# A decoder kernel's mixture stage: the last attention batch's tail dealt over thirteen expert pairs in place of eleven, and TensorE's part of it started one step in instead of three

## The chip, the cores and the metric

The kernel runs on one core of a Trainium2 chip. Each core has engines with queues of their own: TensorE (PE in the rows, its weight loads PEld), VectorE (DVE), ScalarE (ACT), GpSimd (POOL) and SyncE, which issues the transfers (SP). They run their queues in order and wait for each other on semaphores. The metric is the device time in microseconds, lower is better.

## The reference, cut to what matters

The program is a two-layer decoder over 4 batches of 512 tokens, width 128, in fp32. Six sublayers follow each other, each with a residual and a layer norm. The change lies where the second (cross attention, stage b) ends and the third (the mixture of experts, stage c) begins:

```
x = _layernorm(x + _L0_xattn_ref(ctx, x, ...))       # stage b: 16 heads of 64, then out @ Wo
x = _layernorm(x + _L0_ffn_ref(x, ...))              # stage c
...
logits = flat @ router_w.T                           # 16 experts
topk_scores, topk_idx = jax.lax.top_k(logits + router_bias, 2)
hidden = jax.nn.silu(gate_all) * up_all              # every expert, width 64
out = jnp.einsum('nk,nkd->nd', combine, down_all)    # plus one shared expert of width 128
```

## The kernel before, in words

Every engine's queue is written by Python generators. Each stage has a generator for each engine; a `yield` ends a step, and `weave` deals several generators out into one queue in proportion to numbers given by hand: `weave((g, n), (h, m))` takes from the one whose next step is the earlier by (steps taken + 1) / n. `later(n, g)` puts n empty steps ahead of g, `part(g, n)` takes only n steps of g, and `both` chains two.

Stage c works a batch in 9 pairs, p = 0 to 8 (`c_experts_*`). A pair covers two experts: on TensorE a gate and an up matmul, each 512 columns of fp32 (rows `c_gt` and `c_up`; `c_sg` and `c_su` for p = 8), and a matmul that spreads the routing weights over the partitions (`c_sel`, from `c_CT`). ScalarE makes the silu of the gate (`c_SG`, L1286), VectorE multiplies it by the up product (L1303, semaphore `c_su`) and then by the routing weight into `c_H` (L1309, semaphore `c_h`). Four down products per batch follow among the next batch's pairs (`c_dn`, L1329 adds them to X).

Between the pairs stands the routing of the next batch (`c_route_*`): logits (`c_rw`), L1213 and the picks up to L1217 on VectorE, an exp on ScalarE (L1205), then L1221 to L1235 on VectorE, which leave the one-hot weights `c_oh`; TensorE transposes these (L1199), and L1241 and L1243 make `c_CT` of them.

Into batch 0's pairs the tail of stage b is dealt, for the last attention batch (`b_out_*`): VectorE inverts the denominators (L966) and splits them in two fp16 halves (L972, L974, twice, `b_rp`). TensorE spreads them to eight tiles, a = 0 to 7, with two matmuls each (`b_rp,b_sel`); VectorE scales each tile of `b_OT` (L979, semaphore `b_sel`); TensorE multiplies by the output weights (`b_wo,b_OT`, 32 matmuls, semaphore `b_out`); VectorE adds to X and normalises (L236, L191 to L213); TensorE transposes the result (L221), which is needed by the fourth batch's routing and experts only.

PSUM banks come from a ring of six: `take` waits for the last reader of the bank's former content, so where a matmul stands in the queue also decides which semaphore it waits for.

Of the kernel before, what the change touches and what calls it, by code (L numbers as in the profile page):

```python
# [14 lines left out]
NB, T, D, TC = 4, 512, 128, 154  # L15
# [19 lines left out]
def weave(*streams):  # L35

    live = [[g, n, 0] for g, n in streams]
    while live:
        s = min(live, key=lambda s: (s[2] + 1) / s[1])
        s[2] += 1  # L40
        if next(s[0], StopIteration) is StopIteration:
            live.remove(s)


def part(gen, n):
    for _ in range(n):
        if next(gen, StopIteration) is StopIteration:
            return
        yield


def later(n, gen):
    for _ in range(n):
        yield
    yield from gen


def both(first, then):
    yield from first
    yield from then  # L60


def run(gen):
    for _ in gen:
        pass
# [60 lines left out]
def build(nc, io, phases=6):  # L126
    with ExitStack() as ctx:
        sems = {}

        def sem(name):  # L130
            name = SHARED.get(name, (name, 0))[0]
            if name not in sems:
                sems[name] = ctx.enter_context(nc.semaphore(name))
            return sems[name]
# [14 lines left out]
        ring = Ring(6)  # L149
# [8 lines left out]
        def mm(e, out, lhsT, rhs, start=True, stop=True):  # L158
            return e.matmul(out, lhsT, rhs, start=start, stop=stop, skip_group_check=True)  # L159
# [64 lines left out]
        def turn_tensor(t, s, b, banks=ring):  # L224

            bk = banks.take(t, ("turn", s, b), 1, "xt_" + s, b + 1)
            t.wait_ge("xr_" + s, b + 1)
            transpose4(t.e, bk, xb(b)).then_inc(sem("tp_" + s), 1)

        def turn_scalar(a, s, b):  # L230
            a.wait_ge("tp_" + s, b + 1)
            copy(a.e, XT[:, cols(b)], PS[:, bank["turn", s, b], :]).then_inc(sem("xt_" + s), 1)
# [707 lines left out]
        def b_out_tensor(t, b, banks=ringP):  # L940
            e, O = t.e, b_OT[b % 2]
            for _ in range(4):
                yield
            for a in range(8):
                bk = banks.take(t, ("bsel", b, a), 1, "b_sel", 8 * b + a + 1)
                t.wait_ge("b_rt", 2 * b + 2)
                mm(e, PS[:, bk, :], b_sel[:, a, :], b_rp[:, 0, :], stop=False)
                mm(e, PS[:, bk, :], b_sel[:, a, :], b_rp[:, 1, :], start=False).then_inc(sem("b_st"), 1)
                yield
            yield  # L950
            bo = banks.take(t, ("bo", b), 1, "b_add", b + 1)
            t.wait_ge("b_sel", 8 * b + 8)
            for j in range(4):
                for a in range(8):
                    last = mm(e, PS[:, bo, 128 * j:128 * j + 128], O[:, a, 128 * j:128 * j + 128], b_wo[:, a, :],
                              start=(a == 0), stop=(a == 7))
            last.then_inc(sem("b_out"), 1)
            for _ in range(12):
                yield
# [29 lines left out]
        B_OUT = 25  # L989
# [129 lines left out]
                    c_load_sync(s)  # L1119

        def b_tail_tensor(t):
            yield from later(3, b_out_tensor(t, NB - 1, ring))
            for _ in range(6):
                yield
            turn_tensor(t, "B", NB - 1)

        def b_tail_scalar(a):
            yield from later(3 + B_OUT + 6, ())
            turn_scalar(a, "B", NB - 1)

        def b_tail_vector(v):
# [203 lines left out]
        def c_order(lane, route, experts, tail, rows, turn, last, blocks, back):  # L1335


            begun = route(lane, 0)
            for _ in range(3):
                next(begun, None)  # L1340
            second = experts(lane, 1)
            weave((tail, B_OUT + 10), (both(experts(lane, 0, begun), part(second, 2)), 11))
            keys = both(rows(lane, 0), later(7, both(turn(lane, 0), both(blocks(lane), both(rows(lane, 1), later(16, turn(lane, 1)))))))
            weave((both(second, both(experts(lane, 2), experts(lane, 3))), 25), (later(46, keys), 112))
            run(back(lane, 0))
            for j in range(4):
                last(lane, NB - 1, j)
# [1075 lines left out]
        @block.tensor  # L2423
        def _(e):
            t = Lane(e, sem, "pe")
            a_tensor(t)
            b_tensor(t)
            if phases == 2:
                run(b_tail_tensor(t))
                return  # L2430
            c_order(t, c_route_tensor, c_experts_tensor, b_tail_tensor(t), lambda t, m: d_rows_tensor(t, m, ring),
                    lambda t, m: d_turn_tensor(t, m, ring), c_down_tensor, none, none)
            hidden = f_hidden_tensor(t, 0)
            d_order(t, d_chain_tensor, d_prep_tensor, lambda t, m: d_keys(t, d_rows_tensor, d_turn_tensor, m, ringD), d_late_tensor, e_first_tensor,
                    e_attend_tensor, none, c_last_tensor, none, none, lambda t, b: f_route_tensor(t, b, ringD), hidden)
            f_start_tensor(t)
            f_order(t, f_hidden_tensor, hidden, f_route_tensor, none, f_late_tensor)

        @block.scalar
        def _(e):  # L2440
            a = Lane(e, sem, "act")
            a_scalar(a)
            b_scalar(a)
            if phases == 2:
                run(b_tail_scalar(a))
                return
            c_order(a, c_route_scalar, c_experts_scalar, b_tail_scalar(a), d_rows_scalar, d_turn_scalar, none,
                    d_first_scalar, d_back_steps_scalar)
            hidden = f_hidden_scalar(a, 0)
            d_order(a, none, d_prep_scalar, lambda a, m: d_keys(a, d_rows_scalar, d_turn_scalar, m), d_late_scalar, e_first_scalar, e_attend_scalar,  # L2450
                    f_split_scalar, c_last_scalar, d_back_steps_scalar, d_blocks_steps_scalar, f_route_scalar, hidden)
            f_order(a, f_hidden_scalar, hidden, f_route_scalar, none, f_late_scalar)
# [152 lines left out]
```

## Time and profile before

| | us |
|---|---|
| median of 3 runs | 1805.92 |
| lowest, highest | 1803.56, 1810.51 |
| profiled execution, its own time | 1803.57 |
| its span | 1801.8 |
| TensorE busy, of the span | 1551.4 |
| VectorE busy | 1204.8 |
| first routing matmul of stage c starts at | 963.98 |
| stage b's output matmuls (`b_wo`), last batch | 996.58 to 1003.99 |

Times in the rows are microseconds from the span's start. The time lies 1.77 us over the span. A group of the timeline names the engine, the line, the operation and the tiles, output before input; fp32 matmuls count double, since each is run as two passes. In brackets stands how long the engine idled ahead of it and who ended that.

### The profile page before, as it was taken

The page shows a single profiled execution, that of the slowest core. Times are in us where ns is not written, and L with a number is a line of the kernel's source. Part 1 is how long each engine was busy: PE and PEld are TensorE (multiplying, and loading weights), DVE is VectorE, ACT ScalarE, POOL GpSimd, SP SyncE. Part 2 cuts the span into 40 slices and gives each one's busy share as a digit, 9 for nine tenths or more (in the row PEclk, how much of TensorE's full clock was granted, in tenths as well). Part 3 has the DMA queues.
Part 4 walks back from the last instruction along what each step waited for, and adds up shares of the span by engine and source line. Part 5 has one row for each costly group of instructions (what it writes and reads, how often), then busy time and mean ns, then how long its engine had stood idle before and what let it go on. Part 6 is the DMA issues. An engine that isn't in the chain of part 4 may idle for free.

```text
span 1801.8 us, 41198 instructions
## 1 busy us (share of the span) xinstructions
PE 1551.4 (86%) x17764; PEld 801.4 (44%) x17764; DVE 1204.8 (67%) x2337; ACT 907.4 (50%) x1258; POOL 667.7 (37%) x705
## 2 busy tenths in 40 slices
PE   4888877799999999999987888778988999798985
PEld 1222222233334333433422544567777778665542
DVE  6778875677775777567544567665576676565676
ACT  1676664367765776577574133335545444333220
POOL 1110110155654555466473003477555675100000
PEclk9899997799999999999998999999999999969998
DMA  4000002222231322223120100000000001100000
GB/s 146 1 1 1 1 1 79 68 68 83 70 98 53 106 68 68 69 84 89 48 68 13 62 1 1 13 3 15 15 15 15 15 3 47 49 2 1 1 13 12
DMA packets 32406, 70.61 MB, mean 39 GB/s; under 512 B 5328, under 2 KB 7056, under 8 KB 31968
## 3 DMA queue, kind: packets, MB, share of 16 engines
q1 hardware_dynamic: 32224, 67.98, 13.0%
q8 instruction: 140, 2.29, 0.6%
q14 instruction: 42, 0.34, 0.1%
HBM read 47.45 MB, written 20.51 MB: 38 GB/s over the span
## 4 chain that ended last, share of the span: by engine, by line
PE 57%; DVE 26%; ACT 6%; issue 5%; POOL 5%; DMA 1%; SPq 0%; DVEq 0%; ACTq 0%; POOLq 0%
PE ps L159 55%; DVE a_MX L371 4%; DVE b_mx L802 3%; POOL d_XI L1627 2%; POOL d_tmp L1624 2%; PE ps L221 1%; DVE d_KV L1519 1%; DVE b_VL L749 1%; POOL b_EL L874 1%; ACT d_L L162 1%; DVE st L165 1%; ACT d_XE L162 1%; DVE sq L200 1%; DVE st L191 1%; DVE X L197 1%
## 5 line engine op out<-in xcount | busy, mean ns | idle before, releaser
L874 POOL TENSOR_TENSOR b_EL<-b_X,b_EH 128x1024 f16<-128x1024 f32 x160 | 341.3, 2133 | 311.2 <-ACT b_EH L162 311.2
L802 DVE TENSOR_REDUCE b_mx<-ps 128x2 f32<-128x666 f32 x256 | 216.8, 847 | 103.3 <-PE ps L159 103.1
L1624 POOL TENSOR_TENSOR d_tmp<-d_G,d_XI 128x31 f32<-128x31 f32 (+15 forms) x248 | 130.1, 524 | 287.5 <-DVE d_G L1555 268.7
L856 ACT ACTIVATE b_X<-ps 128x1024 f32<-128x1024 f32 x160 | 163.8, 1024 | 131.1 <-PE ps L159 130.1
L162 ACT ACTIVATE b_EH<-b_X 128x1024 f16<-128x1024 f32 x160 | 169.1, 1057 | 27.9 <-PE ps L159 16.7
L408 ACT ACTIVATE a_E<-ps 128x1024 f32<-128x1024 f32 x128 | 131.2, 1025 | 102.8 <-PE ps L159 102.4
L371 DVE TENSOR_REDUCE a_MX<-ps 128x2 f16<-128x1024 f32 x128 | 155.3, 1226 | 39.6 <-PE ps L159 39.4
L159 PE MATMUL ps<-b_M,b_S 128*128 128x512 f16 (+1 forms) x768 | 176.6, 383 | 2.0 <-ACT b_X L856 2.0
L1627 POOL TENSOR_TENSOR d_XI<-d_XI,d_tmp 128x31 f32<-128x31 f32 (+15 forms) x248 | 140.9, 568 | 19.4
L159 PE MATMUL ps<-b_Hk,b_Hq 64*128 64x333 f16 x512 | 83.2, 322 | 39.9 <-DVE b_mx L802 36.9
L390 POOL TENSOR_TENSOR a_QS<-a_QS,a_MR 128x512 f16<-128x512 f16 x16 | 18.5, 1154 | 257.8 <-ACT a_MR L162 257.8
L159 PEld LDWEIGHTS ps<-b_Hk,b_Hq 64*128 64x128 f16 x512 | 24.7, 93 | 165.5 <-DVE b_mx L802 139.3
L159 PEld LDWEIGHTS ps<-b_M,b_S 128*128 128x128 f16 (+1 forms) x768 | 55.4, 97 | 76.7 <-issue 24.4
L2350 POOL TENSOR_TENSOR f_Y<-X,f_bo 128x512 f32<-128x512 f32 x4 | 6.1, 1536 | 202.9 <-DVE X L213 112.7
L159 PE MATMUL ps<-a_QS,a_KS 32*128 32x512 f16 x256 | 53.9, 418 | 27.9 <-DVE a_MX L371 26.8
L159 PE MATMUL ps<-f_XM,f_Wh 128*128 128x512 f16 x256 | 78.0, 387 | 0.0
L159 PE MATMUL ps<-a_E,a_VA 128*32 128x512 f32 x512 | 77.5, 681 | 0.4
L1286 ACT ACTIVATE c_SG<-ps 128x512 f32<-128x512 f32 x36 | 21.5, 597 | 110.2 <-PE ps L159 110.2
L159 PE MATMUL ps<-b_EH,b_VH 128*64 128x512 f16 x320 | 65.3, 404 | 5.0 <-POOL b_EL L874 2.7
L162 ACT ACTIVATE d_UW<-ps 128x512 f32<-128x512 f32 x64 | 38.0, 597 | 60.8 <-PE ps L159 60.6
L159 PE MATMUL ps<-d_KV,d_XE 64*64 64x128 f32 x1024 | 66.3, 279 | 1.2 <-issue 0.9
L159 PE MATMUL ps<-XT,a_w 128*128 128x512 f32 x64 | 47.5, 832 | 18.1 <-DMA ident<-ident 8.9
(305 smaller groups left out, 3321.4 us busy)
## 6 DMA issues: line engine op xcount, KB each, us to landing
b_S<-s_xk SPq DMA_DIRECT2D x48, 336.0 KB, 6.3
b_M<-s_xq SPq DMA_DIRECT2D x48, 256.0 KB, 5.1
s_xk<-b_Hk SPq DMA_DIRECT2D x16, 336.0 KB, 2.2
s_xk<-b_Lk SPq DMA_DIRECT2D x16, 336.0 KB, 2.5
s_xq<-b_Hq SPq DMA_DIRECT2D x16, 256.0 KB, 2.0
s_xq<-b_Lq SPq DMA_DIRECT2D x16, 256.0 KB, 2.0
d_XI<-eye SPq DMA_DIRECT2D x8, 512.0 KB, 3.8
f_w<-f_w SPq DMA_DIRECT2D x1, 2048.0 KB, 8.3
```

The costliest lines, as they stand in the source:

```text
L159: return e.matmul(out, lhsT, rhs, start=start, stop=stop, skip_group_check=True)
L162: return e.activation(out, a, ACT.Copy)
L165: return e.scalar_tensor_tensor(out=out, in0=a, scalar=s, in1=b, op0=op0, op1=op1)
L371: v.e.tensor_reduce(out, PS[:, bk:bk + 2, :], AX, ALU.max).then_inc(sem("a_mx"), 1)
L390: p.e.tensor_tensor(a_QS[G % 4], a_QS[G % 4], a_MR[G % 2], ALU.add).then_inc(sem("a_q2"), 1)
L408: a.e.activation(a_E[c][:, 2 * hp:2 * hp + 2, :], PS[:, bk:bk + 2, :], ACT.Exp, scale=float(D) ** -0.5).then_inc(sem("a_ex"), 1)
L802: v.e.tensor_reduce(out, PS[:, bk:bk + 2, 0:333], AX, ALU.max).then_inc(sem("b_mx"), 1)
L856: a.e.activation(b_X[k % 2], PS[:, bk:bk + 2, :], ACT.Exp, scale=0.125).then_inc(sem("b_ex"), 1)
L874: last = p.e.tensor_tensor(b_EL[k % 6], b_X[k % 2], b_EH[k % 6], ALU.subtract)
L1286: a.e.activation(c_SG[n % 3], PS[:, bank["cgu", b, p], :], ACT.Silu).then_inc(sem("c_sl"), 1)
L1624: e.tensor_tensor(tm, a, x, ALU.mult).then_inc(*p.step())
L1627: last = e.tensor_tensor(z, z, tm, ALU.subtract)
```

## The change

It edits four numbers of the weave and two of the tail. The tail's steps are dealt over 13 pairs (batch 0's nine and four of batch 1) in place of 11; the numbers of the weave behind it are lowered to match. TensorE's tail starts after one empty step in place of three, and ScalarE's copy of the transposed result moves with it; VectorE's tail has no such offset, before or after.

```
 def b_tail_tensor(t):
-    yield from later(3, b_out_tensor(t, NB - 1, ring))
+    yield from later(1, b_out_tensor(t, NB - 1, ring))
...
 def b_tail_scalar(a):
-    yield from later(3 + B_OUT + 6, ())
+    yield from later(1 + B_OUT + 6, ())
...
-    weave((tail, B_OUT + 10), (both(experts(lane, 0, begun), part(second, 2)), 11))
+    weave((tail, B_OUT + 10), (both(experts(lane, 0, begun), part(second, 4)), 13))
...
-    weave((both(second, both(experts(lane, 2), experts(lane, 3))), 25), (later(46, keys), 112))
+    weave((both(second, both(experts(lane, 2), experts(lane, 3))), 23), (later(37, keys), 103))
```

No instruction is added or taken away. On TensorE two things move. This is the first, from batch 1's logits, which stand behind pair 1, to the gate and up matmuls of pair 3 (`b_rp,b_sel` are the tail's spreading matmuls, two for each a; - is before, + is the changed kernel):

```order
 L159 MATMUL ps<-c_rw,XT 128x16 x4
 L159 MATMUL ps<-XT,c_gt 128x512 [waits c_su]
 L159 MATMUL ps<-XT,c_up 128x512
 L159 MATMUL ps<-c_CT_163,c_sel 128x512
-L159 MATMUL ps<-b_rp,b_sel 128x512 x2
 L159 MATMUL ps<-b_rp,b_sel 128x512 [waits b_sel]
 L159 MATMUL ps<-b_rp,b_sel 128x512
 L159 MATMUL ps<-b_rp,b_sel 128x512 [waits b_sel]
 L159 MATMUL ps<-b_rp,b_sel 128x512
-L159 MATMUL ps<-XT,c_gt 128x512 [waits c_su,c_lg]
+L159 MATMUL ps<-XT,c_gt 128x512 [waits c_lg,b_sel]
 L159 MATMUL ps<-XT,c_up 128x512
```

Ahead of these rows four of them stood, and now six do. So the tiles a = 0 to 7 stood as 2, 3, 3 behind pairs 1, 2 and 3; now they stand as 3, 2, 3, and the first matmul of pair 3 waits for `c_lg` (L1213) and an early `b_sel` and no more for `c_su` of pair 2. The second is the transpose L221, which moves from behind batch 1's pair 0 to behind its pair 2.

On VectorE the tail's instructions spread out. This is the place of pair 3, from pair 2's L1309 on; L979 scales the tiles of `b_OT`, and L236 is the tail's addition to X:

```order
 L1309 TENSOR_TENSOR c_H_168<-c_SG_166,ps 128x512 [waits c_wm,c_su]
-L979 TENSOR_TENSOR b_OT_101<-b_OT_101,ps 128x512 [waits b_st] x3
+L979 TENSOR_TENSOR b_OT_101<-b_OT_101,ps 128x512 [waits b_st] x2
 L1303 TENSOR_TENSOR c_SG_165<-c_SG_165,ps 128x512 [waits c_um,c_sl]
 L1309 TENSOR_TENSOR c_H_168<-c_SG_167,ps 128x512 [waits c_wm,c_su]
-L236 TENSOR_TENSOR X<-X,ps 128x512 [waits b_out]
-L191 TENSOR_REDUCE st<-X 128x4 [waits b_add]
-L193 TENSOR_SCALAR st<-st 128x4 [waits dve]
+L979 TENSOR_TENSOR b_OT_101<-b_OT_101,ps 128x512 [waits b_st] x2
 L1221 TENSOR_SCALAR c_wt<-c_wt 128x4 [waits c_ew]
 L1223 RECIPROCAL c_wt<-c_wt 128x4 [waits dve]
```

L979 stood three ahead of pair 3's L1303, and now two; and L236, which waits for `b_out`, stood ahead of L1221 and now doesn't.

Some rows on in the same queue, right behind pair 4's L1309, with pair 5's L1303 and L1309 in it:

```order
+L236 TENSOR_TENSOR X<-X,ps 128x512 [waits b_out]
+L191 TENSOR_REDUCE st<-X 128x4 [waits b_add]
+L193 TENSOR_SCALAR st<-st 128x4 [waits dve]
+L197 TENSOR_TENSOR X<-X,st 128x512 [waits dve]
 L1303 TENSOR_TENSOR c_SG_167<-c_SG_167,ps 128x512 [waits c_um,c_sl]
 L1309 TENSOR_TENSOR c_H_168<-c_SG_166,ps 128x512 [waits c_wm,c_su]
-L180 TENSOR_TENSOR st<-st 128x4 [waits dve]
-L165 SCALAR_TENSOR_TENSOR st<-st 128x4 [waits dve] x2
-L180 TENSOR_TENSOR st<-st 128x4 [waits dve]
-L165 SCALAR_TENSOR_TENSOR st<-st 128x4 [waits dve]
+L200 TENSOR_TENSOR sq<-X 128x512 [waits dve]
+L204 TENSOR_REDUCE st<-sq 128x4 [waits dve]
```

L236, L191 and L193 are here now, behind the whole of L1221 to L1235 and pair 4; L1241 and L1243, which make the next batch's `c_CT`, stand right behind these rows, now after L204 in place of further steps of the norm. Early in the tail one more thing moves: the first L972 and L974, which stood ahead of pair 0's L1303 and the first L1241 and L1243, now stand behind them. From batch 1's pair 2 on the order of each engine is as it was, but for the L221 and its copy on ScalarE. GpSimd's and SyncE's queues do not change.

## Rows read from the trace of the kernel before

**Rows 1.** The page, part 4: the chain that ended last, by engine.

```profile
PE 57%; DVE 26%; ACT 6%; issue 5%; POOL 5%; DMA 1%; SPq 0%; DVEq 0%; ACTq 0%; POOLq 0%
```

**Rows 2.** Waits of TensorE, 964 to 1023: us in total, times, longest.

```profile
PE ps L159 <- DVE c_SG L1303: 4.9, 2, 3.4
...
PE ps L1199 <- DVE c_oh L1235: 3.8, 2, 3.3
```

**Rows 3.** Windows: busy time of each engine by stretch; PEclk is the granted clock.

```profile
958.00:964.90 6.90, 4.43 (x49) 1.86 (x49) 1.35 (x4) 2.17 (x4) 4.85 (x3) 1.00 0.13 25
964.90:968.50 3.60, 3.56 (x6) 0.95 (x5) 2.84 (x23) 1.64 (x3) 0.00 (x0) 0.53 0.30 120
975.60:982.20 6.60, 6.51 (x16) 3.52 (x16) 2.57 (x4) 1.14 (x2) 0.00 (x0) 0.51 0.00 0
982.20:988.90 6.70, 3.34 (x11) 1.28 (x11) 4.54 (x20) 2.43 (x4) 0.00 (x0) 1.00 0.00 0
988.90:992.40 3.50, 3.50 (x8) 0.84 (x7) 0.74 (x2) 0.39 (x1) 0.00 (x0) 0.51 0.00 0
992.40:1006.00 13.60, 10.04 (x71) 7.99 (x69) 4.26 (x10) 0.60 (x1) 0.00 (x0) 1.00 0.07 17
1006.00:1012.60 6.60, 5.29 (x10) 2.09 (x11) 5.58 (x17) 0.60 (x1) 0.00 (x0) 0.50 0.96 334
```

**Rows 4.** Timeline of TensorE and VectorE, 975 to 1004: start, duration, idle before.

```profile
975.69 1.86 PE L159 MATMUL ps<-b_rp,b_sel 128*128 128x512 f16 x4 [0.49 <-DVE b_rp L974]
...
977.35 1.72 PE L159 MATMUL ps<-c_rw,XT 128*128 128x16 f32 x8
...
978.93 2.08 PE L159 MATMUL ps<-XT,c_gt 128*128 128x512 f32 x2
...
980.80 1.68 PE L159 MATMUL ps<-XT,c_up 128*128 128x512 f32 x2
...
982.73 1.47 PE L159 MATMUL ps<-b_rp,b_sel 128*128 128x512 f16 x6
983.37 1.88 DVE L979 TENSOR_TENSOR b_OT<-b_OT,ps 128x512 f32<-128x512 f32 x3 [3.90 <-PE ps L159]
985.17 0.22 DVE L1213 TENSOR_TENSOR c_lg<-ps,c_rb 128x64 f32<-128x64 f32 x1
...
986.74 0.68 DVE L1303 TENSOR_TENSOR c_SG<-c_SG,ps 128x512 f32<-128x512 f32 x1
...
987.56 1.10 PE L159 MATMUL ps<-XT,c_gt 128*128 128x512 f32 x2 [3.36 <-DVE c_SG L1303]
...
990.43 2.40 PE L159 MATMUL ps<-b_rp,b_sel 128*128 128x512 f16 x6
...
992.35 1.29 DVE L979 TENSOR_TENSOR b_OT<-b_OT,ps 128x512 f32<-128x512 f32 x2 [0.16 <-PE ps L159]
993.55 0.68 DVE L1303 TENSOR_TENSOR c_SG<-c_SG,ps 128x512 f32<-128x512 f32 x1
...
994.38 1.10 PE L159 MATMUL ps<-XT,c_gt 128*128 128x512 f32 x2 [1.55 <-DVE c_SG L1303]
...
996.58 7.41 PE L159 MATMUL ps<-b_wo,b_OT 128*128 128x128 f32 x64
```

**Rows 5.** Timeline of the same two engines, 1004 to 1023.

```profile
1004.03 0.69 DVE L236 TENSOR_TENSOR X<-X,ps 128x512 f32<-128x512 f32 x1 [9.20 <-PE ps L159]
...
1005.55 0.16 DVE L1221 TENSOR_SCALAR c_wt<-c_wt 128x4 f32<-128x4 f32 x1
...
1007.31 1.02 PE L1199 MATMUL ps<-ident,c_oh 128*16 128x128 f32 x4 [3.31 <-DVE c_oh L1235]
...
1015.45 1.10 PE L159 MATMUL ps<-XT,c_gt 128*128 128x512 f32 x2 [0.64 <-DVE c_CT L1243]
...
1022.12 0.66 PE L221 MATMUL ps<-ident,X 128*128 128x128 f32 x4
...
1022.61 0.61 PE L159 MATMUL ps<-c_dn,c_H 128*128 128x128 f32 x4
```


## Prediction

> **What bounds the kernel now.** I read the page first. In its chain TensorE has 57% and VectorE 26% [rows 1], so the kernel alternates between TensorE's own work and places where TensorE waits for VectorE; a time is changed only where one of these waits shrinks or grows. Next I asked for TensorE's waits in the stretch that the change touches. Two entries carry it: 4.9 us in two waits for `c_su` (L1303), the longest 3.4, and 3.8 us for `c_oh` (L1235), the longest 3.3 [rows 2]. Then the windows, for the clock: the granted clock is 0.51 from 975.6 to 982.2 and from 988.9 to 992.4, 0.50 from 1006.0 to 1012.6, and 1.00 between [rows 3]. These are the 1.2 and the 2.4 GHz level, and each of these falls comes shortly after TensorE stood idle for 3.3 us or more. So a long wait here is paid twice. An earlier fall, to 0.53 from 964.9, follows a stretch in which TensorE was busy for 4.43 of 6.90 us in several shorter waits [rows 3]. Last the timeline, which says who is in the way of whom.
>
> Pair 3's `c_gt` starts at 987.56 after 3.36 us of idle time, for pair 2's L1303 [rows 4]. That instruction had its operands from 982.4 on, but stood behind three L979 (983.37 to 985.25) and behind L1213 and the picks, so that it ran at 986.74. Pair 4's `c_gt` waits another 1.55 us, for pair 3's L1303 at 993.55, which again stood behind three L979. `b_wo` then runs 996.58 to 1003.99, all at the full clock. After it TensorE waits 3.31 us for `c_oh`: the exp for it was long done, but L1221 stands behind L236, which waits for `b_out`, and behind L191 and L193, so that it ran at 1005.55 [rows 5]. From 1007.31 TensorE works at half clock, and pair 7's `c_gt` starts only at 1015.45.
>
> **Part one: up to `b_wo`.** I replay the queues of the changed kernel with the durations of the rows.
>
> The recast L972 and L974 brings nothing: pair 0's `c_CT` comes some 0.7 us earlier, but both halves of `b_rp` are complete when they were, and TensorE's spreading matmuls need both. They start at 975.7 as before. There are now six of them ahead of `c_rw` in place of four. At half clock a spreading matmul takes 0.415 us (four from 975.69 to 977.35 [rows 4]), so `c_rw` starts at 978.2. It takes the 1.58 us that lay between 977.35 and 978.93, so pair 2's `c_gt` starts at 979.8, which is 0.85 us late. Its `c_su` of pair 1 has come by then, for only one L979 stands ahead of it. Gate and up and `c_sel` took 3.8 us, from 978.93 to the next spreading matmul at 982.73, nearly all at half clock; begun 0.85 us later more of it falls into full clock, and I put its end at 983.3.
>
> Now the gain. Behind pair 2 stand a = 3 and 4 alone. Tile 3 is spread at 983.8, its L979 follows until 984.6, since tiles 1 and 2 were scaled earlier, and L1213 gives `c_lg` at 984.85. Pair 3's `c_gt` needs this and `b_sel` of tile 2, no more pair 2's L1303, and starts at 984.95 in place of 987.56. The picks take the 1.57 us from L1213 to L1303 (985.17 to 986.74 [rows 4]), so pair 2's L1303 runs at 986.2, when its matmuls are long over, and the two L979 of tiles 4 and 5 end at 988.65, held by tile 5, whose matmuls start at 987.1 when the bank is free. Pair 3's L1303 runs 988.65 to 989.3 and pair 4's `c_gt` starts at 989.45, in place of 994.38. Gate to the end of `c_sel` is 2.2 us (994.38 to 996.58), so `b_wo` starts at 991.65; its last `b_sel` comes at 991.2. **Gain up to here: 996.58 - 991.65 = 4.9 us.** 2.6 us of it come from the wait that changes its partner (987.56 to 984.95). The other 2.3 come between the `c_gt` of pairs 3 and 4, 6.8 us before and 4.5 now: 0.9 from six spreading matmuls at full clock (1.47 us) in place of half (2.40 us), 0.7 from gate, up and `c_sel` (987.56 to 990.43, 2.9 us, now 2.2), 0.6 from a wait of 0.95 us in place of 1.55, since fewer L979 stand ahead of pair 3's L1303.
>
> **Part two: from the end of `b_wo` (call it T) to the first `c_dn`.** L1221 to L1235 take 1.65 us (1005.55 to about 1007.2 [rows 5]); they now stand in the 7.4 us in which `b_wo` runs and VectorE idled 9.2 us. Pair 4's L1303 and L1309 go there too. So TensorE goes from `b_wo` straight into the transposes, without the 3.31 us, and has no idle time for the clock to fall on. A pair at full clock is 2.22 us (three of them from 1015.45 to 1022.12, 6.67 us). After 0.44 us of transposes pairs 5 and 6 take until T + 4.9. Pair 7 waits for `c_ct`, and this is the new critical wait. VectorE starts at T with L236, L191 and L193, 1.52 us (1004.03 to 1005.55), and then has seven instructions of 0.69 us (L197, L1303, L1309, L200, L204, L1241, L1243; the size is that of L236 and L1303 in [rows 4, 5]), 4.8 us. With 0.15 us to TensorE's start, pair 7's `c_gt` starts at T + 6.5. Before it was 1015.45 - 1004.03 = 11.4 us behind T. The pairs 7, 8 and 0 behind it then run without a wait, as they did: pair 8's two last VectorE products end at T + 12.8, and `c_dn` comes at T + 6.5 + 6.67 = T + 13.2. L221, 0.49 us on TensorE between 1022.12 and 1022.61, only changes its place; there X is normalised at T + 13.7, while TensorE reaches L221 about T + 22. **Gain: 11.4 - 6.5 = 4.9 us.** The remaining idle time is 1.6 us at one place. I take it as too short for the clock to fall, since after the 1.55 us at 994.38 it stayed at 1.00 [rows 3, 4]; the price if it does fall is about 1.7 us, half of the 3.5 us stretch from 988.9.
>
> **What else moves.** The bank that L221 takes shifts the ring for a few pairs. The new waits there (pair 3 of batch 1 for pair 2's `c_su`, pair 4 for L221's copy) have a `c_dn` of about 2.1 us as cover, so I cost them at nothing; without that cover each would be below 1 us. The copy on ScalarE stands behind pair 2's silu, ahead of a table load; it can make pair 3's silu late by some 0.4 us, which VectorE's idle time there covers. The loads of the next stage wait for `b_out` and so start 4.9 us earlier; their stretch, DMA share 0.96 from 1006.0 on [rows 3], ends long before stage d. Everything from batch 1's pair 3 on keeps its order and moves as a whole.
>
> **Sum.** 4.9 + 4.9 = 9.8 us. Against the profiled execution's own 1803.57 us (span 1801.8) this is 1793.8. That execution was 2.35 us under the median of the runs; against the median, 1805.92, it is **1796.1 us**, 0.54% faster. A change of 0.5%, about what a measurement of this kernel can tell from none, is 9.0 us here: the forecast lies 0.8 us beyond it.
>
> **The rivals.**
>
> *The clock does not come back (slower).* The gains count on full clock for `b_wo` and the pairs behind it. No wait there is over 1.6 us, but before 964.9 shorter waits than that, 2.5 us of 6.9 in sum, were enough for a fall [rows 3]. The changed kernel has waits of 0.7, 0.1 and 0.95 us from 984 to 990, and one of 1.6 later. If TensorE stayed at half clock from `b_wo` up to L221's new place, `b_wo` would cost 7.4 us more and the work behind it (to T + 22, less the 1.6 us wait) 20.4 us more, of which the wait swallows 1.6: 26.2 us against a gain of 9.8, so 1822.3. It decides for slower than before once 9.8 us of full-clock work run at half, and for slower by over 0.5% at 18.8 us. For it speaks the fall at 964.9; against it that TensorE stays busy for some 80% from 984 to 990 (64% then), and that 1.55 us alone changed nothing. Chance 0.08, half of it for the over 0.5%.
> The Trainium skill, "TensorE: Matmul & The Clock Gate", section "A second HAM failure mode: psum-queue depth-cycling", says that frequent short idles between groups of matmuls that cycle through PSUM banks make the clock swing between its two levels; the changed kernel has such short waits, so by that rule it would go this rival's way, to some 1822 us by the same sum. The trace agrees at 964.9, where 4.43 of 6.90 us were busy and the clock went to 0.53, and not after the 1.55 us wait, where it stood at 1.00.
>
> *The first half is lost, within 0.5%.* Part one hangs on small margins: tile 5's matmuls, the exp with its two table loads on ScalarE ahead of pair 3's silu, and the late start of pair 2. If pair 4's `c_gt` is held 2 to 4 us more than I have, for instance because half clock lasts through pair 2 (0.6 us) and falls again in pair 3's stretch as it did at 988.9 (1.8 us), the gain is 5 to 9 us: 1797 to 1801. If only part two works it is 4.9 us, 1801.0. Chance 0.34.
>
> *The move does nothing.* If the slack is eaten later, because a chain that does not pass here sets the end, the time stays 1805.9. Against it: behind 1023 each engine's order is unchanged and nothing waits for a load. Chance 0.06.
>
> *More than forecast.* Six spreading matmuls with no pause could lift the clock ahead of 982.2. `c_rw`, `c_gt` and `c_up` at full clock would bring up to 2 us more: 1794. Chance 0.14, and 0.38 for the forecast proper.
>
> **How the numbers follow.** Faster by over 0.5% is the forecast and the larger gain, 0.38 + 0.14 = 0.52. Within is the lost first half, the move that does nothing, and half of the clock's rival, 0.34 + 0.06 + 0.04 = 0.44. Slower is the other half, 0.04. The range reaches from 1790, the larger gain and two times more the 1.7 us that a stretch of half clock costs, to 1803, where only part two works (1801.0) and one such stretch is added. The forecast's own range is 1794 to 1797.
>
> **What would show it.** In the profile after: pair 3's `c_gt` no more waiting for L1303, near 985; `b_wo` near 991.7; no idle time ahead of L1199 behind `b_wo`; pair 7's `c_gt` 6.5 us behind the end of `b_wo` with 1.6 us of wait for L1243; `c_dn` first near 1012.3 in place of 1022.6; granted clock 1.00 through that stretch. The prediction is wrong if the first two hold and the clock column shows 0.50 behind them, or if they hold and the span does not follow.

## The result, and the profile after

| | before | after |
|---|---|---|
| median of 8 runs each, us | 1806.77 | 1798.49 |
| lowest, highest | 1803.56, 1810.51 | 1789.21, 1802.61 |
| the profiled execution, us (span) | 1803.57 (1801.8) | 1791.45 (1789.5) |
| mean granted clock in it | 0.944 | 0.953 |

The ratio of the times is 0.9936, with a 95% interval from 0.9912 to 0.9960: 0.4% to 0.9% faster. The medians lie 8.3 us apart, the profiled executions 12.1. Forecast were 9.8 us and 1796.1 for the median, 1790 to 1803 as the range, and 1794 to 1797 as the forecast's own range; the median of 1798.49 lies in the wide one and not in the narrow one.

The eight executions lie 7 us apart before and 13 after, and part of what separates two profiled executions lies far from the change: about 320 us in, the one after was already 6.7 us ahead, with the same instructions. So I read the change from the part of the program that it touches. As a mark I use the first and the third L1199, the transposes for batch 1's and batch 3's routing; all that moved lies between them. First the two rows from the timeline of TensorE of the kernel before (start, duration, tile, idle time before), then the three of the kernel after.

```profile
968.92 0.60 PE L1199 MATMUL ps<-ident,c_oh 128*16 128x128 f32 x4 [0.46 <-DVE c_oh L1235]
...
1041.32 0.60 PE L1199 MATMUL ps<-ident,c_oh 128*16 128x128 f32 x4 [0.87 <-DVE c_oh L1235]
```

```profile
965.65 0.60 PE L1199 MATMUL ps<-ident,c_oh 128*16 128x128 f32 x4 [2.11 <-DVE c_oh L1235]
...
993.38 0.60 PE L1199 MATMUL ps<-ident,c_oh 128*16 128x128 f32 x4
...
1025.76 0.60 PE L1199 MATMUL ps<-ident,c_oh 128*16 128x128 f32 x4 [0.88 <-DVE c_oh L1235]
```

From the first to the third it is 1041.32 - 968.92 = 72.4 us before and 1025.76 - 965.65 = 60.1 after: **12.3 us saved, where the forecast had 9.8**. The second L1199 has no idle time ahead of it any more. That the profiled executions as a whole lie 12.1 us apart, nearly the same number, is chance: the one after was 3.3 us ahead at the first mark (965.65 against 968.92) and took 3.2 us more from the third mark to its end (763.7 against 760.5).

The waits of TensorE after, from 961 to 1010 (us in total, times, longest), which answer to [rows 2]:

```profile
PE ps L159 <- DVE c_CT L1243: 4.4, 2, 2.7
PE ps L1199 <- DVE c_oh L1235: 2.1, 1, 2.1
PE ps L159 <- DVE b_rp L974: 1.1, 1, 1.1
PE ps L159 <- DVE c_SG L1303: 0.7, 1, 0.7
PE ps L159 <- DVE c_lg L1213: 0.6, 1, 0.6
```

The 4.9 us for L1303 are 0.7, and the wait for `c_oh` that is left, 2.1, is the one ahead of the first L1199. Two waits grew: pair 7's for `c_CT`, 1.6 of the 4.4 us (before 0.6), and the one for `b_rp`, from 0.5 to 1.1; the first wait for `c_CT` shrank from 3.6 to 2.7. The windows, for the clock (PE, PEld, DVE, ACT and POOL busy, granted clock, DMA share, GB/s), which answer to [rows 3]:

```profile
965.60:971.60 6.00, 2.70 (x9) 1.07 (x9) 5.90 (x10) 0.67 (x2) 0.00 (x0) 1.00 0.00 0
971.60:975.00 3.40, 2.76 (x8) 1.33 (x9) 2.17 (x5) 0.00 (x0) 0.00 (x0) 0.50 0.00 0
975.00:986.13 11.13, 9.82 (x32) 3.79 (x32) 8.75 (x31) 4.56 (x6) 0.00 (x0) 1.00 0.00 0
986.13:993.50 7.37, 7.37 (x67) 7.33 (x67) 2.19 (x8) 0.00 (x0) 0.00 (x0) 1.00 0.01 2
993.50:1006.56 13.06, 11.43 (x31) 4.03 (x28) 12.10 (x30) 2.98 (x5) 0.00 (x0) 1.00 0.62 210
```

Half clock is left in one place, 971.6 to 975.0. Before it lasted twice as long there and came back twice more. And the timeline after, TensorE from the spreading matmuls to the first down products, which answers to [rows 4, 5]:

```profile
970.70 0.39 PE L159 MATMUL ps<-c_CT,c_sel 48*128 48x512 f16 x1 [2.74 <-DVE c_CT L1243]
972.24 2.72 PE L159 MATMUL ps<-b_rp,b_sel 128*128 128x512 f16 x6 [1.15 <-DVE b_rp L974]
974.75 1.09 PE L159 MATMUL ps<-c_rw,XT 128*128 128x16 f32 x8
975.69 1.10 PE L159 MATMUL ps<-XT,c_gt 128*128 128x512 f32 x2
...
979.51 1.10 PE L159 MATMUL ps<-XT,c_gt 128*128 128x512 f32 x2 [0.57 <-DVE c_lg L1213]
...
983.93 1.10 PE L159 MATMUL ps<-XT,c_gt 128*128 128x512 f32 x2 [0.74 <-DVE c_SG L1303]
...
986.13 7.41 PE L159 MATMUL ps<-b_wo,b_OT 128*128 128x128 f32 x64
...
999.89 1.10 PE L159 MATMUL ps<-XT,c_gt 128*128 128x512 f32 x2 [1.64 <-DVE c_CT L1243]
...
1006.56 2.27 PE L159 MATMUL ps<-c_dn,c_H 128*128 128x128 f32 x18
```

Pair 3's `c_gt` now waits 0.57 us and for L1213 in place of 3.36 for pair 2's L1303. It stands 13.9 us behind the first L1199 (before 18.6), pair 4's 18.3 (25.5), and `b_wo` 20.5 (27.7). So the first part brought 7.2 us. From the end of `b_wo`, 986.13 + 7.41 = 993.54, pair 7's `c_gt` is 6.35 us away and `c_dn` 13.0.

### The profile page after: what moved, and what is told of

Read it like the earlier page. It is cut to its first block, busy times and chain, and to the rows that moved or that the text cites. A ratio compares the mean times of both kernels' runs of the same rounds, so it can differ in the third digit from the quotient of the medians.

```text
span 1789.5 us, 41198 instructions
## 1 busy us (share of the span) xinstructions
PE 1546.2 (86%) x17764; PEld 805.1 (45%) x17764; DVE 1205.5 (67%) x2337; ACT 907.3 (51%) x1258; POOL 665.9 (37%) x705
## 4 chain that ended last, share of the span: by engine, by line
PE 58%; DVE 27%; ACT 7%; issue 5%; POOL 3%; DMA 1%; SPq 0%; DVEq 0%; ACTq 0%; POOLq 0%
PE ps L159 56%; DVE a_MX L371 4%; DVE b_mx L802 3%; PE ps L221 1%; POOL d_XI L1627 1%; POOL d_tmp L1624 1%; DVE d_KV L1519 1%; DVE b_VL L749 1%; POOL b_EL L874 1%; DVE st L165 1%; ACT d_L L162 1%; ACT d_XE L162 1%; DVE sq L200 1%; DVE st L191 1%; DVE X L197 1%
## 5 line engine op out<-in xcount | busy, mean ns | idle before, releaser
L162 ACT ACTIVATE b_EH<-b_X 128x1024 f16<-128x1024 f32 x160 | 169.1, 1057 | 27.9 <-PE ps L159 16.7
L1627 POOL TENSOR_TENSOR d_XI<-d_XI,d_tmp 128x31 f32<-128x31 f32 (+15 forms) x248 | 140.1, 565 | 19.4
L159 PE MATMUL ps<-b_Hk,b_Hq 64*128 64x333 f16 x512 | 82.7, 320 | 39.8 <-DVE b_mx L802 36.5
L159 PE MATMUL ps<-a_QS,a_KS 32*128 32x512 f16 x256 | 53.0, 411 | 27.7 <-DVE a_MX L371 26.6
```

The lines of the kernel that those rows point to most:

```text
L162: return e.activation(out, a, ACT.Copy)
L1627: last = e.tensor_tensor(z, z, tm, ALU.subtract)
```

## The experiments

In each of them the program outside the tail's stretch is that of the kernel it is made from. The table has, in us from the first L1199, where `b_wo` and the second and third L1199 start in the profile of each run, and how long the granted clock stayed at 0.5 in the stretch that began near 6.0 us (summed over short windows). The texts behind it take the runs one by one.

| run | made from | `b_wo` | second | third | half clock |
|---|---|---|---|---|---|
| before | | 27.7 | 38.4 | 72.4 | 6.8 |
| after | | 20.5 | 27.7 | 60.1 | 3.4 |
| after, second profile | after | 20.5 | 27.8 | 60.1 | 3.4 |
| after, third profile | after | 20.5 | 27.8 | 60.2 | 3.4 |
| add behind the routing | before | 27.6 | 34.8 | 67.8 | 6.8 |
| add ahead of the routing | after | 20.5 | 31.3 | 65.3 | 3.4 |
| filler in the wait for `c_oh` | before | 27.6 | 38.3 | 73.1 | 6.8 |
| filler ahead of the spreading | before | 29.1 | 39.8 | 73.4 | 10.2 |
| filler in the wait for `c_CT` | after | 20.6 | 27.9 | 60.2 | 3.4 |
| offset one alone | before | 23.6 | 35.8 | 70.4 | 6.8, from 2.5 |
| reciprocal ahead | after | 21.7 | 28.9 | 61.3 | 6.8 |
| more ahead of `c_rw` | before | 28.8 | 39.6 | 73.1 | 10.2 |
| more ahead of `c_rw`, reciprocal ahead | after | 21.1 | 28.4 | 60.8 | 3.4 |
| four edits | after | 21.6 | 28.8 | 59.9 | 6.8 |

The three profiles of the changed kernel agree within 0.1 us in every column, although these executions took 1791.45, 1795.03 and 1789.37 us: the stretch is the same each time, and differences of half a microsecond in it can be read. The kernel before has one profile, but the two kernels made from it that change nothing ahead of `b_wo` have it at 27.6 too, with 6.8 us of half clock. The other edits have one profile each.

The part behind the mark can be read too, from the same profiles. From the third L1199 to the end of the span it is 759.5 to 770.6 us, mean 765.0, in the six made from the kernel before (itself among them), and 758.9 to 770.7, mean 765.5, in the eight made from the changed one. So nothing shows that a later chain takes the gain back, though among such scatter a loss of a few us would not be seen.

**Part two alone.** L236 and what follows it on VectorE moved behind the routing and pair 4's products, TensorE's order left as before.

```diff
             yield
-            yield
+            yield from later(4 if b == NB - 1 else 1, ())
             v.wait_ge("b_out", b + 1)
```

> The kernel before, in which only L236 of the last `b_out` and the products behind it are moved behind pair 4's L1303 and L1309; TensorE's order is that of before. It is part two of the forecast alone. The measure is the distance from the first to the third L1199 of the stretch: 72.4 us in the profile of before, 60.1 in that of the changed kernel. My theory (two parts that add up): the wait for `c_oh` behind `b_wo` goes, 3.3 us, pair 7's `c_gt` comes 6.5 us behind the end of `b_wo` and `c_dn` 13.2 us behind it; the distance shrinks by 4.9 us, to about 67.5, and the whole time by 4.9 us, 0.27%. Rival (the first half brings everything, and part two's gain is eaten by the wait for `c_ct`): distance 72.4 to 71, whole time unchanged. Rival (half clock behind `b_wo` comes from the work of before it and not from the 3.3 us wait): half clock still shows from the transposes on, and pair 7 comes later than 8 us behind the end of `b_wo`.

Measured: ratio to before 0.9969 [0.9947, 0.9992], medians 1800.92 and 1806.28; the distance shrank by 4.6 us. TensorE from the end of `b_wo` on in this run:

```profile
990.06 7.41 PE L159 MATMUL ps<-b_wo,b_OT 128*128 128x128 f32 x64
997.31 0.60 PE L1199 MATMUL ps<-ident,c_oh 128*16 128x128 f32 x4
...
1004.42 1.10 PE L159 MATMUL ps<-XT,c_gt 128*128 128x512 f32 x2 [2.24 <-DVE c_CT L1243]
```

The wait for `c_oh` is gone, and pair 7 starts 7.1 us behind the second L1199 (after: 999.89 - 993.38 = 6.5). The 0.6 us more is three short VectorE instructions (L207, L174, L176) that stand ahead of L1241 in this order and behind L1243 in the changed kernel. My theory held (4.6 us for 4.9, pair 7 at 7.0 us behind the end of `b_wo` for 6.5), and both rivals fall.

**Part one alone.** The changed kernel with L236, L191 and L193 put back ahead of L1221.

```diff
                 e.tensor_tensor(O[:, a, :], O[:, a, :], PS[:, bank["bsel", b, a], :], ALU.mult).then_inc(sem("b_sel"), 1)
-                yield
-            yield
+                yield from later(0 if a == 7 and b == NB - 1 else 1, ())
+            yield from later(0 if b == NB - 1 else 1, ())
             v.wait_ge("b_out", b + 1)
```

> The changed kernel, with L236, L191 and L193 of the last `b_out` put back ahead of L1221, so that the routing waits for `b_wo` again. It is part one of the forecast alone. Forecast by its own sum: `b_wo` starts as early as in the changed kernel, the 3.3 us wait for `c_oh` is back with half clock behind it, and the distance from the first to the third L1199 is 72.4 less 4.9, 67.5 us (65 if part one is worth the 7.2 us that the profile after showed). Rival (part one's larger worth was an accident of that one execution's clock): 67.5 or more, with half clock up to about 982. Rival (the wait for `c_oh` alone carries the whole gain): 70 or more. Whole time 0.3% to 0.4% under before by my theory.

Measured: ratio to before 0.9964 [0.9941, 0.9988], medians 1797.27 and 1806.28; the distance 65.3, 7.1 us less than before. Behind `b_wo` it is the kernel before again:

```profile
994.79 1.02 PE L1199 MATMUL ps<-ident,c_oh 128*16 128x128 f32 x4 [3.31 <-DVE c_oh L1235]
```

The windows of TensorE in this run (busy, granted clock, DMA share, GB/s) over `b_wo` and the wait, and over what follows:

```profile
984.06:993.40 9.34, 7.41 (x65) 1.00 0.09 14
993.50:999.90 6.40, 5.11 (x10) 0.50 0.99 325
```

Part one is thus 7.1 us and part two 4.6, and 0.6 comes from having both (the three short instructions above): 12.3. That part one was worth more than 4.9 is no accident of one execution. By the whole times alone the two parts can't be told apart: 0.9969 and 0.9964.

**Is the wait for `c_oh` paid twice?** The kernel before, with TensorE kept at work in that wait.

```diff
-            t.wait_ge("c_oh", b + 1)
+            [mm(e, PS[:, bk, :], b_sel[:, 0, :], b_rp[:, 0, :]) for _ in range(14 * (b == 1))]; t.wait_ge("c_oh", b + 1)
```

> The kernel before, with 14 matmuls of 128 columns more, into the bank that the transposes will overwrite, ahead of the last wait for `c_oh`, so that TensorE is busy for part of that wait; their result is overwritten. If half clock behind `b_wo` comes from the idle 3.3 us, the granted clock stays at 1.00 from there on and the pairs behind take 2.2 us each in place of 2 x that: `c_dn` comes some 2 to 3 us nearer to the end of `b_wo` than in before (18.6 us), at 15.5 to 16.5. If half clock comes for another reason (the work ahead), the clock falls to about 0.5 all the same and the distance stays at 18.6 us or more.

```profile
1002.26 3.18 PE L159 MATMUL ps<-b_rp,b_sel 128*128 128x512 f16 x14
1005.73 0.60 PE L1199 MATMUL ps<-ident,c_oh 128*16 128x128 f32 x4 [0.29 <-DVE c_oh L1235]
...
1013.04 1.10 PE L159 MATMUL ps<-XT,c_gt 128*128 128x512 f32 x2 [2.43 <-DVE c_CT L1243]
```

The windows of the same run: the filled wait, pairs 5 and 6, and a stretch behind pair 7's start.

```profile
1002.30:1005.70 3.40, 3.14 (x16) 1.00 0.60 167
1005.70:1010.70 5.00, 4.88 (x14) 1.00 1.00 353
1014.40:1017.80 3.40, 3.40 (x6) 0.50 0.01 2
```

The added matmuls have 512 columns, as the rows show, and not the 128 that the expectation names. The clock theory held in this run: with the wait filled the fall behind `b_wo` is gone and pairs 5 and 6 ran at full clock. The gain that I expected of it did not come: `c_dn` starts 19.4 us behind the end of `b_wo`, where I had 15.5 to 16.5 and before it was 18.6. From the start of `b_wo` to pair 7's `c_gt` it is 18.0 us in place of 1015.45 - 996.58 = 18.9, because TensorE then waited 2.43 us for L1243 in place of 0.64; and behind that wait the clock fell once more, so that the whole distance came out 0.7 us longer. Up to pair 7, half clock behind `b_wo` cost the kernel before 0.8 us, since VectorE's chain to `c_CT` was right behind it. What part two gains, it gains for the most part by bringing that chain forward.

**The profile again.** No edit.

> The changed kernel once more, for a second profile. The profile after showed half clock only from 971.9 to 974.7 where I had forecast it until about 982, and `b_wo` 5.4 us earlier than forecast. Theory of the six spreading matmuls (they lift the clock because nothing interrupts them): again full clock from about the end of the first six on, and 20.5 us from the first L1199 to `b_wo`. Rival (where the clock turns is an accident of the execution): a different length of half clock, with the distance up to 25 us. Distance from the first to the third L1199: 60.1 by the first, 60 to 64 by the second.

The distance is 60.1, half clock 3.4 us long, `b_wo` at 20.5, one execution of 1795.03 us. The rival, an accident of the execution, falls. (Of the 5.4 us by which the expectation has `b_wo` too early, 3.3 lie ahead of the first L1199; by the mark it is 2.2.) Whether the six matmuls are the cause was still open.

**What decides how long half clock lasts?** Before and after begin to spread within 0.2 us of each other, and the one is at half clock twice as long. First the short gap ahead of the spreading matmuls in the kernel before, filled:

```diff
-                t.wait_ge("b_rt", 2 * b + 2)
+                [mm(e, PS[:, bk, :], c_sel[0:48, 0, :], b_sel[0:48, 0:4, :]) for _ in range(1 * (b == NB - 1 and a == 0))]; t.wait_ge("b_rt", 2 * b + 2)
```

> The kernel before, with one matmul of 512 columns more between the `c_sel` of pair 1 and the four spreading matmuls, in the 0.4 us in which TensorE waits there for `b_rp`; it writes the bank that the spreading matmuls overwrite. In before TensorE is at half clock for 6.9 us from 6.0 us behind the first L1199, in the changed kernel for 3.4 us only, though both begin to spread within 0.2 us of each other. Theory A (what TensorE does in the gap ahead of the spreading matmuls decides how long half clock lasts): with the gap filled the clock is back about 9.3 us behind the first L1199, as in the changed kernel, `c_rw` takes 1.1 us in place of 1.72 and pair 2's `c_gt` 1.1 in place of 2.08, so that `c_sel` of pair 2 ends some 2 us sooner. Theory B (it is the six in a row in place of four, or the earlier `c_sel`): half clock lasts until about 12.9 as before. In both pair 3's `c_gt` still waits for L1303, since that instruction stands behind three L979; its wait grows by what is won ahead of it under A only as far as VectorE isn't brought forward: distance from the first L1199 to `b_wo` 25.5 to 27.6.

Theory A is wrong, and B didn't foresee this either. `b_wo` came at 29.1, outside the 25.5 to 27.6 that I had for both, and the windows of TensorE show 10.2 us of half clock with the engine busy all through, and full clock only while it was idle again.

```profile
968.70:978.90 10.20, 10.20 (x24) 0.50 0.00 0
979.00:982.20 3.20, 0.42 (x2) 1.00 0.00 0
```

Next the long wait ahead of it in the changed kernel, filled:

```diff
-                    t.wait_ge("c_ct", b + 1)
+                    [mm(e, PS[:, 6, :], c_sel[0:48, 0, :], b_sel[0:48, 0:4, :]) for _ in range(10 * (b == 0 and k == 0))]; t.wait_ge("c_ct", b + 1)
```

> The changed kernel, with ten matmuls of 512 columns more (2.1 us) in the 2.7 us in which TensorE waits for the first `c_CT`; they write the bank that `c_sel` overwrites. If the fall of the clock 6.0 us behind the first L1199 comes from the idle time there, it goes: the six spreading matmuls take 1.5 us in place of 2.7, and `b_wo` starts 0.5 to 1.2 us sooner, 19.3 to 20 us behind the first L1199 in place of 20.5 (pair 2's `c_gt` can't start ahead of pair 1's L1303). If the clock falls all the same, 20.5.

The ten matmuls ran 2.33 us, which left 0.47 us of that wait and the 1.15 for `b_rp`. The clock fell all the same, at the same place, and nothing moved (distance 60.2). So the long wait isn't needed for this fall.

Then the six spreading matmuls 0.8 us sooner, by one reciprocal of the four placed ahead of the routing:

```diff
-                if q % 2:
+                if q % 2 or (b == NB - 1 and q == 0):
                     yield
...
-            begun = route(lane, 0)
+            begun = route(lane, 0); lane.name == "dve" and next(tail)
```

> The changed kernel with the first of the four L966 (0.85 us each) moved ahead of L1213, into the 0.77 us in which VectorE waits for the routing's matmuls. If what TensorE then waits for is VectorE's chain from the first L1235 to `b_rp`, `c_CT` and `b_rp` both come 0.8 us sooner and `b_wo` too: 19.7 us behind the first L1199 in place of 20.5, and the distance from the first to the third L1199 59.3 in place of 60.1. Rival (the clock then turns at another place, or the next wait takes it up): 60 to 62.

```profile
966.58 0.39 PE L159 MATMUL ps<-c_CT,c_sel 48*128 48x512 f16 x1 [1.92 <-DVE c_CT L1243]
968.11 2.62 PE L159 MATMUL ps<-b_rp,b_sel 128*128 128x512 f16 x6 [1.15 <-DVE b_rp L974]
970.53 1.73 PE L159 MATMUL ps<-c_rw,XT 128*128 128x16 f32 x8
972.10 2.05 PE L159 MATMUL ps<-XT,c_gt 128*128 128x512 f32 x2
```

Both waits ended 0.8 us sooner, as forecast, and the stretch came out 1.2 us longer: half clock lasted 6.8 us, with six spreading matmuls in a row as in the changed kernel. So the six in a row are not what brings the clock back early; my reading of the first profile falls, and the rival (the clock turns at another place) is right. The run gives a free test besides: it is the changed kernel with the long half clock that the prediction assumed. The prediction's 22.7 us to `b_wo`, less the 0.8, is 21.9, and 21.7 was measured.

The last theory was that `c_rw`, if it runs within the first part of half clock, keeps it long. Four matmuls more ahead of `c_rw` push it out, once in the kernel before and once in the run just told:

```diff
-            bk = ring.take(t, ("clg", b), 1, "c_lg", b + 1)
+            bk = ring.take(t, ("clg", b), 1, "c_lg", b + 1); [mm(e, PS[:, bk, :], c_sel[0:48, 0, :], b_sel[0:48, 0:4, :]) for _ in range(4 * (b == 1))]
```

> The kernel before, with four matmuls of 512 columns more between the four spreading matmuls and `c_rw` (8 in a row in place of 4). So far half clock lasted 3.4 us in the runs in which TensorE did only spreading matmuls until it ended (`c_rw` from 9.1 us behind the first L1199 on), and 6.8 or 10.2 in those in which `c_rw`, eight matmuls' records of 16 columns, ran ahead of that point (from 8.2 to 8.5 on), also with six spreading matmuls in a row. Theory C (`c_rw` inside the half-clock stretch keeps it long): with `c_rw` pushed to 9.3 us the clock is back at about 9.4, and pair 2's `c_gt` starts at 10.2 and takes 1.1 us. Rival D (the idle time ahead decides, which is as in before): half clock lasts 6.8 us or more and pair 2's `c_gt` starts at 10.9 and takes 2.1.

> The run with one reciprocal moved forward, and four matmuls of 512 columns more between the six spreading matmuls and `c_rw`, so that `c_rw` starts at 9.0 to 9.1 us behind the first L1199 in place of 8.2. Theory C: half clock lasts 3.4 us in place of 6.8, and `b_wo` starts 20.4 us behind the first L1199 in place of 21.7; distance from the first to the third L1199 60.0. Rival D: half clock lasts 6.8 us again and `b_wo` comes 0.5 to 0.8 us later than without them, at 22.2 to 22.5, distance 61.9 to 62.2.

In the kernel before it fails: `c_rw` starts at 10.4 us and half clock lasts 10.2.

```profile
979.50:989.70 10.20, 9.84 (x22) 0.50 0.00 0
```

Pair 3's `c_gt` then waited 3.36 us, as long as in the kernel before, and here the clock stayed at 1.00, from 989.8 to 1010.0:

```profile
994.63 1.10 PE L159 MATMUL ps<-XT,c_gt 128*128 128x512 f32 x2 [3.36 <-DVE c_SG L1303]
```

In the other it holds: half clock was 3.4 us long in place of 6.8, and `b_wo` came 0.5 us sooner than without the four, work added and time won, though at 21.1 and not at the 20.4 that I had. Windows of TensorE in that run:

```profile
973.50:976.90 3.40, 3.40 (x9) 0.50 0.00 0
977.00:988.00 11.00, 9.69 (x34) 1.00 0.00 0
```

Theory C explains one of two and is not enough. What decides between 3.4, 6.8 and 10.2 us of half clock stays open.

**One of the change's two choices alone.** The diff has five numbers of the weave and two of the tail, but only two choices stand behind them: thirteen pairs, and the offset of one step. Here is the offset with the eleven pairs of before.

```diff
-            yield from later(3, b_out_tensor(t, NB - 1, ring))
+            yield from later(1, b_out_tensor(t, NB - 1, ring))
...
-            yield from later(3 + B_OUT + 6, ())
+            yield from later(1 + B_OUT + 6, ())
```

> The kernel before with TensorE's and ScalarE's steps of the end of stage B one ahead in place of three, and the eleven pairs of before. VectorE's order is that of before. Tile 0 is now spread ahead of pair 1's `c_gt`, so that pair 1 waits until `b_rp` is there, 6.6 us behind the first L1199 in place of 0.4. By my theory (the two numbers only work together) this alone loses: pair 1's work, 1.9 us and its `c_su`, all comes behind `b_rp`, with half clock, and the first half is 1 to 4 us longer than before: 28.5 to 31.5 us from the first L1199 to the end of what stands ahead of `b_wo`; distance from the first to the third L1199 73 to 77. Rival (the offset is what gains): below 70.

```profile
970.66 1.04 PE L159 MATMUL ps<-b_rp,b_sel 128*128 128x512 f16 x2 [6.08 <-DVE b_rp L974]
971.49 1.92 PE L159 MATMUL ps<-XT,c_gt 128*128 128x512 f32 x2
```

Pair 1 waits 6.1 us, as I had said, and still the distance is 70.4, 2.0 us less than before and not more. The step that was wrong: I put all that follows at half clock. The clock fell 2.5 us behind the first L1199, inside the 6.1 us of idle time, where half clock costs nothing, and from 9.4 to 19.6 us all ran at the full one; and `b_wo` went ahead of pair 4, at 23.6, partly at half clock again (8.72 us for 7.41). So the offset alone gains 2.0 of the 12.3 us, in one profile. The other half, thirteen pairs with the old offset, was not tried, so what it would do alone stays open.

**Toward a better version.** The reciprocal as above; L1241 and L1243 ahead of L200 and L204; and both waits ahead of the spreading matmuls filled.

```diff
-            yield from normalize(v, xb(b), 1e-5, "xr_B", fine=True)
+            yield from (x for i, _ in enumerate(normalize(v, xb(b), 1e-5, "xr_B", fine=True)) for x in range(3 if b == NB - 1 and i == 1 else 1))
...
-                t.wait_ge("b_rt", 2 * b + 2)
+                [mm(e, PS[:, bk, :], c_sel[0:48, 0, :], b_sel[0:48, 0:4, :]) for _ in range(5 * (b == NB - 1 and a == 0))]; t.wait_ge("b_rt", 2 * b + 2)
...
-                    t.wait_ge("c_ct", b + 1)
+                    [mm(e, PS[:, 6, :], c_sel[0:48, 0, :], b_sel[0:48, 0:4, :]) for _ in range(8 * (b == 0 and k == 0))]; t.wait_ge("c_ct", b + 1)
```

> The changed kernel with four edits more: one L966 ahead of L1213; L1241 and L1243 of batch 1's table ahead of L200 and L204, so that pair 7's wait of 1.6 us for `c_CT` shrinks to 0.2; and 8 and 5 matmuls of 512 columns more in the waits for the first `c_CT` (1.9 us) and for `b_rp` (1.15 us), so that TensorE is nearly never idle between the first L1199 and the spreading matmuls. If the clock stays at 1.00 with both waits filled: `c_sel` 4.2 and spreading 5.8 us behind the first L1199, `b_wo` at 18.6 to 19.3 in place of 20.5, pair 7's `c_gt` 5.0 us behind the end of `b_wo` in place of 6.35, and a distance from the first to the third L1199 of 56.8 to 57.6 in place of 60.1. If the clock falls there all the same (as it did with the first wait alone filled): `b_wo` at 20.4 to 21.7, distance 58.7 to 60. Whole time 1.5 to 3 us under the changed kernel, too little to be told in the ratio.

> The changed kernel, timed beside the one with four edits more. Ratio to before 0.991 to 0.996 as in the first comparison, median 1797 to 1800; distance from the first to the third L1199 60.1 us, half clock there 3.4 us long.

Timed together: with four edits more 0.9919 [0.9889, 0.9949] of before, median 1787.81 of 6 runs; the changed kernel 0.9930 [0.9908, 0.9952], median 1790.17 of 10; before 1804.44. The intervals overlap, so the ratios don't tell the two apart. For the changed kernel the ratio, the distance and half clock came as expected; the median, for which I had 1797 to 1800, came 7 us lower. In the stretch the edits cancel. Pair 7's wait is 0.31 us, so the table ahead of the square brought its 1.3 us:

```profile
997.29 1.10 PE L159 MATMUL ps<-XT,c_gt 128*128 128x512 f32 x2 [0.31 <-DVE c_CT L1243]
```

But `b_wo` came at 21.6 in place of 20.5. With both waits filled TensorE was busy for 3.55 of the 3.64 us ahead, and the clock fell and stayed down for 6.8 us:

```profile
965.51:969.15 3.64, 3.55 (x16) 1.00 0.00 0
969.20:972.60 3.40, 3.40 (x13) 0.50 0.00 0
972.60:976.00 3.40, 3.40 (x6) 0.50 0.00 0
```

Of the four, L1241 and L1243 ahead of the square is the one to keep; alone on the changed kernel it was not run.

## Why the prediction was right

**The ratio.** Forecast 0.54% faster, measured 0.64%, by medians 8.3 us for 9.8. The forecast's chance of 0.52, for faster by over 0.5%, lay on the side that came, but narrowly: the interval reaches from 0.4% to 0.9%, and the medians taken by themselves give 0.46%. The mark in the trace says 12.3 us. The two comparisons (0.9936 and 0.9930, 11.6 and 12.6 us) agree with it, but their intervals hold the forecast's 9.8 as well, so it is the mark alone that tells the two apart. By it, what came is the rival "more than forecast" (0.14) and not the forecast proper (0.38).

**Part one, the mechanism.** Each step came where it was put: `c_rw` behind six spreading matmuls, pair 3's `c_gt` held by L1213 and no more by pair 2's L1303, pair 4's `c_gt` 4.4 us behind it (forecast 4.5), held by L1303 for 0.7 us (forecast 0.95).

**Part one, the size.** The mis-sized term is the clock: the prediction kept half clock up to about 982, as before, and so had pair 3's `c_gt` 16.0 us behind the first L1199 and `b_wo` 22.7; measured were 13.9 and 20.5. Half clock lasted 3.4 us and not 6.8, so `c_rw`, gate and up of pair 2 ran at the full clock. That is 2.2 us in three profiles of three, the size that the rival "more than forecast" gave it (up to 2). Its reason, six spreading matmuls with no pause, is refuted as a cause by itself by the run with the reciprocal ahead. So part one is 7.1 for the forecast 4.9, and the sum 12.3 for 9.8; of the 2.5 us that the sum is short, this one term is 2.2. That the clock is its cause is shown by the run with the reciprocal ahead, which has the long half clock and comes out at the prediction's sum.

**Part two.** Forecast 4.9 us, pair 7's `c_gt` at 6.5 behind the end of `b_wo` and `c_dn` at 13.2, with 1.6 us of wait for L1243. Measured 6.35, 13.0 and 1.64, and 4.6 for the part alone, 5.2 on top of part one (65.3 to 60.1). The prediction's opening said that "a long wait here is paid twice". For this one that was wrong in effect: the filled wait took the half clock away and gained 0.8 us up to pair 7. The sum didn't rest on it, since it was taken from VectorE's chain. The reading behind it, that each fall comes shortly after 3.3 us or more of idle time, doesn't hold either: behind `b_wo` the clock fell at 1006.0, 2.0 us into the wait; near 6.0 us behind the first L1199 it fell also with the waits there filled (four edits); and with four matmuls more ahead of `c_rw` in the kernel before, pair 3's 3.36 us of idle time left it at 1.00.

**The rivals.** The clock that does not come back did not happen: after waits of 0.57, 0.74 and 1.64 us the granted clock stayed at 1.00 up to 1006.56. The Trainium skill's section "A second HAM failure mode: psum-queue depth-cycling" in "TensorE: Matmul & The Clock Gate" would have it swing there; in this stretch it did not. The first half was not lost, which had 0.34; the move did not do nothing.

## What to carry to other kernels

Where one engine waits for an instruction that was ready long before it ran, look at what stands ahead of it in its queue: changing which instruction a wait hangs on (3.4 us to 0.6), and moving a chain into the time another engine's long matmul leaves idle (3.3 us to none), can be priced by replaying the queues. The second part was worth what the replay said (4.6 to 5.2 us for 4.9); the first was worth 2.2 us more (7.1 for 4.9), because the replay had to assume when the clock comes back. A half clock or a wait is worth removing only if the next engine isn't right behind it; replay that one too before counting it. And where executions scatter by more than the edit is worth, compare distances between two marks in the traces: here these agreed within 0.1 us over three profiles while the eight times of the changed kernel lay up to 13 us apart.

## What the runs showed of the hardware that was not expected

- Near the change, stretches of half clock came out 3.4, 6.8 or 10.2 us long in these profiles, and a small edit changed which: six spreading matmuls begun 0.8 us sooner turned 3.4 into 6.8 (`b_wo` 1.2 us later), and four useless matmuls more turned that back to 3.4 (`b_wo` 0.5 us sooner).
- In these runs a busy TensorE wasn't safe from the fall. With 3.55 of 3.64 us busy, mostly matmuls that contract over 48 rows, the clock fell (four edits); with 3.14 of 3.40 us busy, with matmuls over 128 rows, it stayed at 1.00 (filler in the wait for `c_oh`). Both runs in which half clock lasted 10.2 us also had added matmuls over 48 rows within it. But in the run with the reciprocal and four matmuls more over 48 rows, the first of these also began within half clock (975.82, the stretch ended near 976.9), and it lasted 3.4 us. What makes the difference is open: what stood ahead differed as well, and no two kinds of filler were run in the same wait.
- Behind `b_wo`, waits of 1.64 us (after) and 2.24 (part two alone) left the clock at 1.00; behind one of 2.43 (filler in the wait for `c_oh`) it fell. The length of the wait isn't the whole of it: of two waits of 3.36 us for pair 3's `c_gt` the clock fell behind the one (before, at 988.9) and stayed at 1.00 behind the other (more ahead of `c_rw` in before).
